# Four normalizations of every 128-row tile issued on ScalarE with scale and bias, and GpSimd computing the bias

## Chip, cores and metric

The kernel runs on one core of a Trainium2 chip. The metric is the device time of one launch in microseconds (us). The engines are named as in the profile: PE is TensorE (PEld its weight loads), DVE is VectorE, ACT is ScalarE, POOL is GpSimd, SP is SyncE, which here issues all DMAs.

## What is computed

One transformer layer over x of shape 16 x 1024 x 256, with two residual branches, each closed by a layer norm without weights:

```
x = x + layernorm(attention(layernorm(x)))     # 16 heads of 16, relative-position scores, softmax over 1024 keys
x = x + layernorm(ffn(layernorm(x)))           # base + shared rank 16 + 6 routed experts of rank 16, top 2 by softmax
layernorm(x) = (x - mean(x)) / sqrt(var(x) + 1e-5)    # over the 256 columns
```

So there are four normalizations for each row: before attention (xn here), after attention (yn), before the ffn (xn1), after the ffn (y2n).

## The kernel before

Rows are taken in 128 tiles of 128 rows, 8 tiles for each of 16 batches. A tile t of attention runs in 16 **groups** g = 0 to 15: four key blocks jp = g // 4 of 256 keys, and in each four slices i = g % 4 of 32 query rows. A group is a fixed round over the engines:

- PE computes the scores of the group in two halves (`scores`, L662 content term from `qm` and keys, L667 position term from `rm` and the table `tw`). Between the halves it transposes the maxima of the group before (L674).
- DVE takes the maxima (`maxima`, L962, writes r), then reduces the transposed ones (`spread`, L971 writes nm, L974 writes nmm).
- PE then does other work of the tile (`wide`, `mixed`): probabilities times values (L693), transposes (L700, L705), projections (L714), and then subtracts the maximum by a matmul with nmm (`shift`, L683).
- ACT takes the exponential of the shifted scores (`before`, L847), one group later.

The work that belongs to other tiles is hung into these groups at fixed places: the projections of tile n = t + 8, the output projection and first residual of tile t - 1 (a), the ffn of tile t - 2 (b). The order on every engine is written out by hand, and semaphores join them; each engine works strictly in its own order. The prologue projects 8 tiles without attention, the main loop is unrolled over 3 tiles (42 passes, so 126 tiles), and two short tiles close.

POOL's order in one tile (function `tile` of the gpsimd block) is, from group 12 on: bias add of y (L612) and y2 (L615), `rstd` for rs1 and rs3 (L541 to L543: variance plus eps, then the power -0.5, on one column), the residual x1 (L625), `mask(0)`, `rstd` for rs2, `mask(1)`, `mask(2)`, the output residual res (L641), and in the next tile `mask(3)`, the fp16 splits of x1T and xT (L547, L549), `rstd` for rs0, the products wp of the attention parts with their weights (L580) and their sums (L588, L590), the bias add qkb (L594) and the split into qkh and qkl (L547, L549). `mask(i)` (L534, L535) prepares `qm` and `rm` of the next tile; PE asks for it before the scores of group i.

DVE's side work (`side`) holds, besides the statistics (L923, L925), the four normalizations `normal` (L928), a tensor_scalar that subtracts the mean and multiplies by rs: xn in group 3, yn in 13, y2n in 14, xn1 in 15. In group 5 it holds the gate of the ffn's router, among it L1005 (gate), L1010 (ceq) and L1011 (cgt).

What asks for the four results: PE transposes xn and xn1 in group 0 (L705), POOL adds yn in x1 and y2n in res, and SP loads the next x tile once xn is written.

Of the kernel before, what the change touches and what calls it, by code (L numbers as in the profile page):

```python
# [13 lines left out]
P = 128  # L14
# [24 lines left out]
def sandwich_kernel(nc, x, wqT, bq, wkT, bk, wvT, bv, woT, bo, relT, baseT, base_b,  # L39
                    shAT, shBT, roAT, roBT, rtT, rtb, out):  # L40
    f32, f16 = mybir.dt.float32, mybir.dt.float16
    ALU = mybir.AluOpType
    ACT = mybir.ActivationFunctionType
# [9 lines left out]
    with ctx:  # L53
        def sb(name, shape, dt=f32):
            return ctx.enter_context(nc.sbuf_tensor(name, shape, dt))
# [11 lines left out]
        tri = sb("tri", [P, E, E])  # L67
        mhalf = sb("mhalf", [P, 1])
        eps = sb("eps", [P, 1])
        one = sb("one", [P, 1])  # L70
# [48 lines left out]
        xin = sb("xin", [P, D])  # L119
        xn = sb("xn", [P, D])  # L120
# [3 lines left out]
        mv0 = sb("mv0", [P, 2])  # L124
        ve0 = sb("ve0", [P, 1])
        rs0 = sb("rs0", [P, 1])
        qkf = sb("qkf", [P, 4, P])
        qkb = sb("qkb", [P, 4, P])
# [7 lines left out]
        y = sb("y", [P, D])  # L136
# [8 lines left out]
        ve1 = sb("ve1", [P, 1])  # L145
        rs1 = sb("rs1", [P, 1])
        st2 = sb("st2", [P, 6])
        mv2 = sb("mv2", [P, 2])
        ve2 = sb("ve2", [P, 1])
        rs2 = sb("rs2", [P, 1])  # L150
        st3 = sb("st3", [P, 6])
        mv3 = sb("mv3", [P, 2])
        ve3 = sb("ve3", [P, 1])
        rs3 = sb("rs3", [P, 1])
        hf = sb("hf", [P, NH])
        lg = sb("lg", [P, E])
# [333 lines left out]
        def _(pool):  # L490
# [7 lines left out]
            g.memset(tri[:, :, :], 1.0)  # L498
            g.memset(mhalf[:, :], -0.5)
            g.memset(eps[:, :], EPS)  # L500
            g.memset(one[:, :], 1.0)
# [37 lines left out]

            def rstd(dst, mv, ve):  # L540
                g.tensor_tensor(ve[:, :], mv[:, 1:2], eps[:, :], ALU.add)  # L541
                pool.drain()
                return g.tensor_tensor(dst[:, :], ve[:, :], mhalf[:, :], ALU.pow)  # L543

# [12 lines left out]
            def tile(t, n, att, proj, a, b, ph=None):  # L557
# [12 lines left out]
                if proj:  # L570
                    pool.wait_ge(s_xT, n + 1)
                    split([flat(xT2[:, k, :, :]) for k in range(2)], flat(xT[:, :, :]), s_xT2)

                    pool.wait_ge(s_mv0, n + 2)
                    rstd(rs0, mv0, ve0).then_inc(s_rs0, 1)
                if a:
# [39 lines left out]
                if a:  # L616
                    pool.wait_ge(s_mv1, t)
                    rstd(rs1, mv1, ve1).then_inc(s_rs1, 1)
                if b:
                    pool.wait_ge(s_mv3, t - 1)  # L620
                    rstd(rs3, mv3, ve3).then_inc(s_rs3, 1)
                if a:
# [8 lines left out]
                if a:  # L631
                    pool.wait_ge(s_mv2, t)
                    rstd(rs2, mv2, ve2).then_inc(s_rs2, 1)
                if att:
# [8 lines left out]
            pool.wait_ge(s_mv0, 1)  # L643
            rstd(rs0, mv0, ve0).then_inc(s_rs0, 1)
            passes(pool, tile)


# [185 lines left out]
        def _(act):  # L833
# [4 lines left out]
            def copy(dst, src):  # L838
                return A(dst, src, ACT.Copy)  # L839

            def exp(g, buf, count, free):

                jp, i = divmod(g, NI)
                act.wait_ge(s_shift, count)
                if not (isinstance(free, int) and free <= 0):
                    act.wait_ge(s_pv, free)
                A(prob[:, jp % 2, :, :, i * IW:(i + 1) * IW],  # L847
                  sc[:, 2 * buf:2 * buf + 2, :].rearrange("p c (h i) -> p c h i", i=IW),
                  ACT.Exp).then_inc(s_exp, 1)

            def before(g, t, ph):

                pg = (g - 1) % NG
                exp(pg, buffer(ph, g - 1), t * NG + g, (t - 1 if g == 0 else t) * NJP + pg // NI - 1)

            def tile(t, n, att, proj, a, b, ph=None):
                for g in range(NG):
# [55 lines left out]
                    if a if g == 0 else att:  # L913
                        before(g, t, ph)

            passes(act, tile)


        @block.vector
        def _(dve):  # L920
# [6 lines left out]
            def normal(dst, src, mv, rs):  # L927
                return v.tensor_scalar(dst, src, mv[:, 0:1], rs[:, 0:1], ALU.subtract, ALU.mult)  # L928
# [48 lines left out]
            def side(g, t, n, proj, a, b):  # L977
# [9 lines left out]
                if g == 2 and proj:  # L987

                    dve.wait_ge(s_x, (n + 1) * 16)
                    stats(st0, mv0, xin[:, :]).then_inc(s_mv0, 1)  # L990
                if g == 3 and proj:
                    dve.wait_ge(s_rs0, n + 2)
                    dve.wait_ge(s_xTp, n + 1)
                    normal(xn[:, :], xin[:, :], mv0, rs0).then_inc(s_xn, 1)
                if g == 4 and b:
# [54 lines left out]
                if g == 13 and b:  # L1050
                    dve.wait_ge(s_y2, t - 1)
                    stats(st3, mv3, y2[:, :]).then_inc(s_mv3, 1)
                if g == 13 and a:
                    dve.wait_ge(s_rs1, t)
                    normal(yn[:, :], y[:, :], mv1, rs1).then_inc(s_yn, 1)
                if g == 14 and a:
                    dve.wait_ge(s_x1, t)
                    stats(st2, mv2, x1[:, :]).then_inc(s_mv2, 1)
                if g == 14 and b:
                    dve.wait_ge(s_rs3, t - 1)  # L1060
                    normal(y2n[:, :], y2[:, :], mv3, rs3).then_inc(s_y2n, 1)
                if g == 15 and a:
                    dve.wait_ge(s_rs2, t)
                    normal(xn1[:, :], x1[:, :], mv2, rs2).then_inc(s_xn1, 1)

# [43 lines left out]
```

## Time and profile before

| | |
|---|---|
| time, median of 3 runs | 6342.19 us (6337.41 to 6345.55) |
| the profiled execution | 6342.86 us |
| its span | 6341.1 us |
| busy: PE, DVE, POOL, ACT | 94%, 79%, 58%, 49% |
| mean granted TensorE clock | 0.985 |

The span is the time from the first to the last recorded instruction; 1.8 us of the execution lie outside it. Rows of the trace are given as start in us, duration in us, engine, line, operation, output <- inputs, shapes and count; a bracket at the end is the time in which the engine stood idle just before, and what ended it.

### The profile page before, as it was taken

Reading aid. Unit: us, or ns where it says so; the run is one execution under the profiler, and the core shown is the slowest. Engines: PE = TensorE matmul, PEld = TensorE weight load, DVE = VectorE, ACT = ScalarE, POOL = GpSimd, SP = SyncE. Lnnn points to the kernel's source line nnn. Section 1 sums busy time; section 2 is a strip of 40 time slices with the busy share of each in tenths; the row PEclk is TensorE's granted clock in tenths of the full one; section 3 lists DMA queues with packets and bytes.
Section 4 is the critical chain, followed back from the end, with each engine's and each line's share of the span. In section 5 each row is a group of like instructions: output and inputs, shape, how many; then the busy total and the mean of one; then the engine's idle time right before and its main releaser. Section 6 shows DMA issues by size and latency. Waiting matters only on the chain.

```text
span 6341.1 us, 408511 instructions
## 1 busy us (share of the span) xinstructions
PE 5961.8 (94%) x178176; PEld 5617.6 (89%) x178176; DVE 4987.0 (79%) x10289; ACT 3127.8 (49%) x5145; POOL 3652.9 (58%) x4709
## 2 busy tenths in 40 slices
PE   5999999999999999999999999999999999999997
PEld 4989899899998998898999899899999999998987
DVE  3787788878788887878887888888788788887786
ACT  1555455455555554555555555455555555554554
POOL 5555655565565555555655655555565556556555
PEclk7999999999999999999999999999999999999998
DMA  3111121111212112121121211112111121211211
GB/s 87 39 44 52 36 61 36 54 44 38 60 36 62 36 36 62 36 61 34 42 58 36 60 37 49 47 40 60 36 53 45 36 60 40 59 37 36 62 36 27
DMA packets 570090, 296.74 MB, mean 47 GB/s; under 512 B 384177, under 2 KB 534689, under 8 KB 568625
## 3 DMA queue, kind: packets, MB, share of 16 engines
q1 hardware_dynamic: 568624, 272.86, 16.0%
q8 instruction: 1450, 23.76, 1.6%
q14 instruction: 16, 0.12, 0.0%
HBM read 184.46 MB, written 88.60 MB: 43 GB/s over the span
## 4 chain that ended last, share of the span: by engine, by line
PE 83%; DVE 8%; issue 4%; DVEq 3%; POOLq 1%; ACT 1%; POOL 0%; SPq 0%; DMA 0%
PE sc L667 22%; PE pw L693 15%; PE sc L683 14%; PE sc L662 13%; PE pm L714 4%; PE pw L700 4%; PE pw L714 4%; PE pm L674 4%; DVE r L962 3%; DVEq L973 2%; DVE y2n L928 2%; DVE nm L971 1%; PE pm L727 1%; PE pm L705 1%; DVE gate L1005 1%
## 5 line engine op out<-in xcount | busy, mean ns | idle before, releaser
L962 DVE TRANSPOSE_TENSOR_REDUCE r<-sc 128x32 f16<-128x1024 f32 x2048 | 2548.8, 1245 | 52.0 <-PE sc L667 51.4
L667 PE MATMUL sc<-rm,tw 96*128 96x32 f16 x65536 | 2293.4, 177 | 71.6 <-issue 70.8
L847 ACT ACTIVATE prob<-sc 128x1024 f32<-128x1024 f32 x2048 | 2097.3, 1024 | 193.7 <-PE sc L683 141.3
L667 PEld LDWEIGHTS sc<-rm,tw 96*128 96x128 f16 x65536 | 1979.9, 97 | 79.5 <-issue 79.0
L662 PE MATMUL sc<-qm,ks 96*128 96x64 f16 x32768 | 1639.8, 193 | 28.8 <-DMA ks<-qk_s 15.5
L971 DVE TENSOR_REDUCE nm<-pm 16x32 f16<-16x256 f32 x2048 | 840.8, 411 | 753.7 <-PE pm L674 750.3
L662 PEld LDWEIGHTS sc<-qm,ks 96*128 96x128 f16 x32768 | 1302.8, 98 | 34.3 <-issue 34.2
L683 PE MATMUL sc<-nmm,pick 128*128 128x64 f16 x32768 | 1302.0, 193 | 2.5 <-DVE nmm L974 1.2
L683 PEld LDWEIGHTS sc<-nmm,pick 128*128 128x128 f16 x32768 | 1151.9, 98 | 122.4 <-issue 105.5
L693 PE MATMUL pw<-prob,vs 128*32 128x128 f32 x32768 | 1115.7, 277 | 129.8 <-DVE nm L971 124.7
L693 PEld LDWEIGHTS pw<-prob,vs 128*32 128x32 f32 x32768 | 842.6, 110 | 185.8 <-DVE nm L971 137.4
L974 DVE TENSOR_TENSOR nmm<-nm,mask_h 16x64 f16<-16x64 f16 x2048 | 607.6, 297 | 195.1 <-issue 9.8
L839 ACT ACTIVATE ot<-pw 128x512 f32<-128x512 f32 x512 | 305.8, 597 | 739.7 <-PE pw L693 739.7
L547 POOL TENSOR_TENSOR oT<-oT,one 128x256 f16<-128x256 f32 x128 | 78.6, 614 | 926.9 <-ACT oT L839 926.9
L535 POOL TENSOR_TENSOR rm<-raw,mask_r 96x512 f16<-96x512 f16 x515 | 608.3, 1181 | 0.0
L534 POOL TENSOR_TENSOR qm<-raw,mask_q 96x512 f16<-96x512 f16 x515 | 591.3, 1148 | 20.3 <-PE sc L667 10.4
L674 PE MATMUL pm<-ident,r 128*128 128x128 f16 x4096 | 561.5, 218 | 0.5 <-DVE r L962 0.5
L839 ACT ACTIVATE nmt<-pm 128x16 f32<-128x16 f32 x512 | 94.2, 184 | 771.1 <-PE pm L727 771.1
L700 PE MATMUL pw<-ident,ot 128*128 128x128 f32 x2048 | 322.9, 280 | 54.2 <-DVE nm L971 53.9
L839 ACT ACTIVATE parts<-pw 128x272 f32<-128x272 f32 x512 | 203.5, 397 | 327.2 <-PE pw L700 320.6
L580 POOL TENSOR_TENSOR wp<-parts,wst 128x1088 f32<-128x1088 f32 x128 | 281.6, 2200 | 113.3 <-ACT parts L839 113.3
L543 POOL TENSOR_TENSOR rs<-ve,mhalf 128x1 f32<-128x1 f32 x521 | 287.4, 552 | 74.0
(131 smaller groups left out, 5803.9 us busy)
## 6 DMA issues: line engine op xcount, KB each, us to landing
raw<-qk_s SPq DMA_DIRECT2D x774, 64.0 KB, 2.8
tw<-tw_s SPq DMA_DIRECT2D x512, 72.0 KB, 2.1
v_s<-vpad SPq DMA_DIRECT2D x136, 256.0 KB, 3.6
vs<-v_s SPq DMA_DIRECT2D x64, 512.0 KB, 3.7
ks<-qk_s SPq DMA_DIRECT2D x384, 64.0 KB, 2.5
xin<-x SPq DMA_DIRECT2D x138, 128.0 KB, 2.9
qk_s<-qkh SPq DMA_DIRECT2D x272, 64.0 KB, 1.7
qk_s<-qkl SPq DMA_DIRECT2D x272, 64.0 KB, 1.6
```

The source lines that it names most:

```text
L534: g.tensor_tensor(qm[:, i, :, :], src, mask_q[:, :, :], ALU.mult)
L535: g.tensor_tensor(rm[:, i, :, :, :].rearrange("p i h s -> p h i s"), src.rearrange("p h (i s) -> p h i s", s=2), mask_r[:, :, :].rearrange ...
L662: last = mm(bank[:, 2 * h * IW:(2 * h + 2) * IW], ks[:, h, j:j + P], qm[:, i, 2 * h:2 * h + 2, :].rearrange("p h i -> p (h i)"), start=(h ...
L667: last = mm(out3[:, :, 2 * k:2 * k + 2], tw[:, jp, u:u + P], rm[:, i, k, :, :], start=False, stop=False, skip_group_check=True)
L674: last = mm(p_max[:, c * P:(c + 1) * P], r1[:, c * H:c * H + P], ident16[:, :], start=True, stop=True)
L683: last = mm(pairs[:, :, h, :], pick[:, h, :], nmm[:, :, :], start=False, stop=True, skip_group_check=True)
L693: last = mm(pw[32 * q:32 * q + 32, col * P:(col + 1) * P], vs[:, 2 * jp + c, h, :], prob[:, jp % 2, c, h, :], start=(c == 0), stop=(c == 1))
L839: return A(dst, src, ACT.Copy)
L847: A(prob[:, jp % 2, :, :, i * IW:(i + 1) * IW], sc[:, 2 * buf:2 * buf + 2, :].rearrange("p c (h i) -> p c h i", i=IW), ACT.Exp).then_inc(s ...
L962: v.tensor_reduce(r1[:, 0:2 * H], sc[:, 2 * buf:2 * buf + 2, :].rearrange("p c (h i) -> p (c h) i", i=IW), axis=AX.X, op=ALU.max, apply_tr ...
L971: v.tensor_reduce(part, p_max[0:H, :].rearrange("h (q i) -> h i q", i=IW), axis=AX.X, op=ALU.max, negate=True).then_inc(s_nmr, 1)
L974: v.tensor_tensor(nmm[0:H, :, :], part.rearrange("h (a i) -> h a i", a=1) .to_broadcast((H, 2, IW)), mask_h[:, :, :], ALU.mult).then_inc(s ...
```

## The change

The four `normal` calls leave DVE and become ACT activations `Identity(scale * x + bias)` with scale = rs and bias = nb, both one column of 128 partitions. Since nb = -mean * rs must be known, the helper `rstd` on POOL now has four instructions in place of two: ng = mean * -1 beside the variance plus eps, and after the power a second drain and nb = ng * rs. Its semaphore is raised after nb. The first normalization of all, ahead of the prologue, stays on DVE. On ACT each normalization stands at the end of its group, behind the exponential.

```
             def rstd(dst, mv, ve, ng, nb):
                 g.tensor_tensor(ve[:, :], mv[:, 1:2], eps[:, :], ALU.add)
+                g.tensor_tensor(ng[:, :], mv[:, 0:1], minus[:, :], ALU.mult)
                 pool.drain()
-                return g.tensor_tensor(dst[:, :], ve[:, :], mhalf[:, :], ALU.pow)
+                g.tensor_tensor(dst[:, :], ve[:, :], mhalf[:, :], ALU.pow)
+                pool.drain()
+                return g.tensor_tensor(nb[:, :], ng[:, :], dst[:, :], ALU.mult)
...
+            def normal(dst, src, rs, nb):          # scalar block
+                return A(dst, src, ACT.Identity, scale=rs[:, 0:1], bias=nb[:, 0:1])
...
                     if a if g == 0 else att:
                         before(g, t, ph)
+                    if g == 3 and proj:
+                        act.wait_ge(s_rs0, n + 2)
+                        act.wait_ge(s_xTp, n + 1)
+                        normal(xn[:, :], xin[:, :], rs0, nb0).then_inc(s_xn, 1)
+                    if g == 13 and a:
+                        act.wait_ge(s_rs1, t)
+                        normal(yn[:, :], y[:, :], rs1, nb1).then_inc(s_yn, 1)
+                    if g == 14 and b:
+                        act.wait_ge(s_rs3, t - 1)
+                        normal(y2n[:, :], y2[:, :], rs3, nb3).then_inc(s_y2n, 1)
+                    if g == 15 and a:
+                        act.wait_ge(s_rs2, t)
+                        normal(xn1[:, :], x1[:, :], rs2, nb2).then_inc(s_xn1, 1)
...
-                if g == 13 and a:                  # vector block; the other three likewise
-                    dve.wait_ge(s_rs1, t)
-                    normal(yn[:, :], y[:, :], mv1, rs1).then_inc(s_yn, 1)
```

On POOL, from the statistics of y2 (group 13) to mask(1), the third tile of the loop before (names: x is the residual x1; ve, rs carry the number of their norm in the code):

```order
L541 TENSOR_TENSOR ve<-mv,eps 128x1
L543 TENSOR_TENSOR rs<-ve,mhalf 128x1
L625 TENSOR_TENSOR x<-yn,xr 128x256
...
L534 TENSOR_TENSOR qm<-raw,mask_q 96x512
L535 TENSOR_TENSOR rm<-raw,mask_r 96x16x16x2
L541 TENSOR_TENSOR ve<-mv,eps 128x1
L543 TENSOR_TENSOR rs<-ve,mhalf 128x1
```

and the same place of the changed kernel:

```order
L551 TENSOR_TENSOR ve<-mv,eps 128x1
L552 TENSOR_TENSOR ng<-mv,minus 128x1
L554 TENSOR_TENSOR rs<-ve,mhalf 128x1
L556 TENSOR_TENSOR nb<-ng,rs 128x1
L638 TENSOR_TENSOR x<-yn,xr 128x256
...
L544 TENSOR_TENSOR qm<-raw,mask_q 96x512
L545 TENSOR_TENSOR rm<-raw,mask_r 96x16x16x2
L551 TENSOR_TENSOR ve<-mv,eps 128x1
L552 TENSOR_TENSOR ng<-mv,minus 128x1
L554 TENSOR_TENSOR rs<-ve,mhalf 128x1
L556 TENSOR_TENSOR nb<-ng,rs 128x1
```

Two instructions more stand ahead of x1 and two more ahead of mask(1); two more still, not shown, stand ahead of wp in the next tile.

On DVE, groups 13 and 14 of the same tile before:

```order
L923 BN_STATS st<-y 128x6
L925 BN_AGGR mv<-st 128x2
L928 TENSOR_SCALAR yn<-y,mv,rs 128x256
L971 TENSOR_REDUCE nm<-pm 16x32
L974 TENSOR_TENSOR nmm<-nm,mask_h 16x64
L961 REGISTER_ALU
L962 TENSOR_REDUCE r<-sc 128x32
L923 BN_STATS st<-x 128x6
L925 BN_AGGR mv<-st 128x2
L928 TENSOR_SCALAR y2n<-y,mv,rs 128x256
```

and on ACT, groups 13 to 15 of the changed kernel, where they have gone:

```order
L863 ACTIVATE prob<-sc 128x32x32
L855 ACTIVATE yn<-y,nb,rs 128x256
L852 ACTIVATE ot<-pw 128x512
L860 REGISTER_ALU
L863 ACTIVATE prob<-sc 128x32x32
L855 ACTIVATE y2n<-y,nb,rs 128x256
L852 ACTIVATE parts<-pw 128x272
L860 REGISTER_ALU
L863 ACTIVATE prob<-sc 128x32x32
L855 ACTIVATE xn<-x,nb,rs 128x256
```

The three normalizations stand between ACT's exponentials and its copies out of PSUM; here xn is the buffer xn1.

## Rows read from the trace of the kernel before

**Rows 1.** The page: the chain that ended last, shares by engine.

```profile
PE 83%; DVE 8%; issue 4%; DVEq 3%; POOLq 1%; ACT 1%; POOL 0%; SPq 0%; DMA 0%
```

**Rows 2.** Waits of PE over the whole span: total us, times, longest.

```profile
PE pw L693 <- DVE nm L971: 124.7, 126, 1.1
...
PE pw L700 <- DVE nm L971: 53.9, 127, 0.5
```

**Rows 3.** Timeline of PE, group 15 to group 6 of the next tile; ACT in group 15.

```profile
3055.11 0.66 PE L700 MATMUL pw<-ident,ot 128*128 128x128 f32 x4 [0.40 <-DVE nm L971]
...
3057.71 0.38 PE L705 MATMUL pm<-ident,xn 128*128 128x128 f32 x2
...
3058.39 0.40 PE L662 MATMUL sc<-qm,ks 96*128 96x64 f16 x8
...
3075.87 1.08 PE L693 MATMUL pw<-prob,vs 128*32 128x128 f32 x32 [1.05 <-DVE nm L971]
...
3056.27 1.02 ACT L847 ACTIVATE prob<-sc 128x1024 f32<-128x1024 f32 x1
```

**Rows 4.** Timeline of DVE in the same stretch.

```profile
3054.04 0.68 DVE L928 TENSOR_SCALAR y2n<-y,mv,rs 128x256 f32<-128x256 f32 x1
...
3068.49 1.03 DVE L974 TENSOR_TENSOR nmm<-nm,mask_h 16x64 f16<-16x64 f16 x1
...
3073.73 0.41 DVE L1005 TENSOR_SCALAR gate<-eg,rg 128x6 f32<-128x6 f32 x1
...
3074.34 1.15 DVE L1011 TENSOR_TENSOR cgt<-gate 128x36 f32<-128x36 f32 x1
3075.41 0.41 DVE L971 TENSOR_REDUCE nm<-pm 16x32 f16<-16x256 f32 x1
```

**Rows 5.** Timeline of POOL in the same stretch.

```profile
3050.70 0.27 POOL L541 TENSOR_TENSOR ve<-mv,eps 128x1 f32<-128x1 f32 x1 [1.71 <-DVE mv L925]
3051.11 0.55 POOL L543 TENSOR_TENSOR rs<-ve,mhalf 128x1 f32<-128x1 f32 x1
3051.63 0.73 POOL L625 TENSOR_TENSOR x<-yn,xr 128x256 f32<-128x256 f32 x1
...
3056.54 1.27 POOL L535 TENSOR_TENSOR rm<-raw,mask_r 96x512 f16<-96x512 f16 x1
...
3066.04 0.19 POOL L541 TENSOR_TENSOR ve<-mv,eps 128x1 f32<-128x1 f32 x1
...
3067.25 2.24 POOL L580 TENSOR_TENSOR wp<-parts,wst 128x1088 f32<-128x1088 f32 x1 [0.32 <-ACT parts L839]
...
3073.08 1.04 POOL L547 TENSOR_TENSOR qkh<-qkb,one 128x512 f16<-128x512 f32 x1 [0.20 <-issue]
3074.27 1.17 POOL L549 TENSOR_TENSOR qkl<-qkb,qkh 128x512 f16<-128x512 f32 x1
```

**Rows 6.** Timelines of the next tile, behind the loop's back edge: PE, then POOL.

```profile
3106.23 0.44 PE L667 MATMUL sc<-rm,tw 96*128 96x32 f16 x11 [1.22 <-issue]
...
3115.24 0.19 POOL L541 TENSOR_TENSOR ve<-mv,eps 128x1 f32<-128x1 f32 x1 [1.96 <-DVE mv L925]
...
3117.59 2.16 POOL L580 TENSOR_TENSOR wp<-parts,wst 128x1088 f32<-128x1088 f32 x1 [1.47 <-ACT parts L839]
```

**Rows 7.** Groups by line: busy us, mean ns, idle before.

```profile
L580 POOL TENSOR_TENSOR wp<-parts,wst 128x1088 f32<-128x1088 f32 x128 | 281.6, 2200 | 113.3 <-ACT parts L839 113.3
...
L839 ACT ACTIVATE y<-pm 128x256 f32<-128x256 f32 x256 | 98.4, 384 | 316.5 <-PE pm L714 316.5
...
L839 ACT ACTIVATE nmt<-pm 128x16 f32<-128x16 f32 x512 | 94.2, 184 | 771.1 <-PE pm L727 771.1
...
L888 ACT ACTIVATE eg<-lg,nlm 128x6 f32<-128x6 f32 x128 | 37.2, 291 | 0.5 <-DVE nlm L999 0.5
```

**Rows 8.** Timelines where POOL is idle: DVE in the last tile, POOL in the prologue.

```profile
6327.93 0.19 DVE L1011 TENSOR_TENSOR cgt<-gate 128x36 f32<-128x36 f32 x1
...
58.81 1.04 POOL L594 TENSOR_TENSOR qkb<-qkf,b_qk 128x512 f32<-128x512 f32 x1 [2.67 <-ACT qkf L839]
```

More of the change, by code:

```diff
@@ L68, in sandwich_kernel @@
         mhalf = sb("mhalf", [P, 1])
+        minus = sb("minus", [P, 1])
         eps = sb("eps", [P, 1])
@@ L126, in sandwich_kernel @@
         rs0 = sb("rs0", [P, 1])
+        ng0 = sb("ng0", [P, 1])
+        nb0 = sb("nb0", [P, 1])
         qkf = sb("qkf", [P, 4, P])
@@ L146, in sandwich_kernel @@
         rs1 = sb("rs1", [P, 1])
+        ng1 = sb("ng1", [P, 1])
+        nb1 = sb("nb1", [P, 1])
         st2 = sb("st2", [P, 6])
@@ L150, in sandwich_kernel @@
         rs2 = sb("rs2", [P, 1])
+        ng2 = sb("ng2", [P, 1])
+        nb2 = sb("nb2", [P, 1])
         st3 = sb("st3", [P, 6])
@@ L154, in sandwich_kernel @@
         rs3 = sb("rs3", [P, 1])
+        ng3 = sb("ng3", [P, 1])
+        nb3 = sb("nb3", [P, 1])
         hf = sb("hf", [P, NH])
@@ L499, in _ @@
             g.memset(mhalf[:, :], -0.5)
+            g.memset(minus[:, :], -1.0)
             g.memset(eps[:, :], EPS)
@@ L538, in mask, with rstd @@
                                 ALU.mult).then_inc(s_mask, 1)
-            def rstd(dst, mv, ve):
+            def rstd(dst, mv, ve, ng, nb):
                 g.tensor_tensor(ve[:, :], mv[:, 1:2], eps[:, :], ALU.add)
+                g.tensor_tensor(ng[:, :], mv[:, 0:1], minus[:, :], ALU.mult)
                 pool.drain()
-                return g.tensor_tensor(dst[:, :], ve[:, :], mhalf[:, :], ALU.pow)
+                g.tensor_tensor(dst[:, :], ve[:, :], mhalf[:, :], ALU.pow)
+                pool.drain()
+                return g.tensor_tensor(nb[:, :], ng[:, :], dst[:, :], ALU.mult)
             def split(two, whole, inc):
@@ L574, in tile @@
                     pool.wait_ge(s_mv0, n + 2)
-                    rstd(rs0, mv0, ve0).then_inc(s_rs0, 1)
+                    rstd(rs0, mv0, ve0, ng0, nb0).then_inc(s_rs0, 1)
                 if a:
@@ L617, in tile @@
                     pool.wait_ge(s_mv1, t)
-                    rstd(rs1, mv1, ve1).then_inc(s_rs1, 1)
+                    rstd(rs1, mv1, ve1, ng1, nb1).then_inc(s_rs1, 1)
                 if b:
                     pool.wait_ge(s_mv3, t - 1)
-                    rstd(rs3, mv3, ve3).then_inc(s_rs3, 1)
+                    rstd(rs3, mv3, ve3, ng3, nb3).then_inc(s_rs3, 1)
                 if a:
@@ L632, in tile @@
                     pool.wait_ge(s_mv2, t)
-                    rstd(rs2, mv2, ve2).then_inc(s_rs2, 1)
+                    rstd(rs2, mv2, ve2, ng2, nb2).then_inc(s_rs2, 1)
                 if att:
@@ L643, in _ @@
             pool.wait_ge(s_mv0, 1)
-            rstd(rs0, mv0, ve0).then_inc(s_rs0, 1)
+            rstd(rs0, mv0, ve0, ng0, nb0).then_inc(s_rs0, 1)
             passes(pool, tile)
@@ L990, in side @@
                     stats(st0, mv0, xin[:, :]).then_inc(s_mv0, 1)
[L991 to L994, printed above, removed]
                 if g == 4 and b:
@@ L1058, in side @@
                     stats(st2, mv2, x1[:, :]).then_inc(s_mv2, 1)
[L1059 to L1064, printed above, removed]
             def tile(t, n, att, proj, a, b, ph=None):
```

## Prediction

> **What bounds the kernel now.** I read the chain that ended last first: PE holds 83% of it, DVE 8% [rows 1]. So PE's own work sets most of the time, and a change elsewhere can act only where PE stands idle or would come to. The waits of PE name two such places that recur in every tile, both on DVE's nm: before the value products L693, 124.7 us in 126 waits (1.0 us each), and before the transposes L700, 53.9 us in 127 (0.42 us each) [rows 2]. The timeline puts L700 into group 15 and the L693 wait into group 6 [rows 3].
>
> What makes DVE late is read on DVE's own rows. In group 14's side work it is y2n, 0.68 us long from 3054.04 [rows 4]; the nm for which PE waits until 3055.11 [rows 3] stands right behind it. In group 5 it is cgt, a 36-element operation that takes 1.15 us and ends at 3075.49; nm follows, and PE goes on at 3075.87 [rows 3, 4]. The same cgt takes 0.19 us in the last tile, where POOL is idle [rows 8]. In the middle of the kernel it ends with POOL's qkl (3074.27 to 3075.44), gate before it ends at 3074.14 with POOL's qkh (3074.12), and nmm at 3069.52 with POOL's wp (3069.49) [rows 4, 5]. So certain DVE operations don't get through while POOL's runs, and DVE's lateness in groups 4 to 6 is that of POOL's queue.
>
> That makes POOL's queue the thing to look at, although POOL is busy only 58% of the span. From the statistics of y2 in group 13 (ve at 3050.70) through x1, three masks, res, mask(3), two splits and rs0 to wp at 3067.25 it is one string of work whose only gap is 0.32 us, ahead of wp, where it waits for ACT's parts [rows 5]. Behind the back edge of the loop PE loses time that nothing shown explains (1.22 us in one piece), and there POOL has gaps of 1.96 and 1.47 us [rows 6]. The mean gap ahead of wp, 113.3/128 = 0.89 us [rows 7], is that of one such tile in three and two tiles with 0.33: (84 x 0.33 + 42 x 2.0)/128 = 0.87. So 84 tiles have 0.33 us of slack in POOL's string, and 42 have enough.
>
> **The change, part by part.**
>
> *DVE loses y2n.* With the 0.68 us out of the way nm comes by up to that much earlier, more than the stall of 0.42 us, so the stall goes. Where POOL isn't the bound that is worth 0.42 us a tile; late next is PE itself. The removal of yn, xn1 and xn gives nothing: PE's waits have no entry for them in the loop.
>
> *ACT gains four activations.* An ACT copy of 256 columns takes 384 ns. The operand columns cost something: eg, six columns wide with a bias column, takes 291 ns, nmt, sixteen wide without, 184 ns [rows 7], about 0.115 us a column. Estimate: 0.384 + 2 x 0.115 = 0.61 us each, between 0.38 and 0.70. ACT is busy 49% and idles around the exponentials, so 2.4 us more a tile fit in. The tightest is xn1, behind the exponential of group 14: PE's second pair of L705 at 3057.71 [rows 3] would be asked for at 3057.31 once the stall is gone, and xn1 would be written at about 3057.5 (the exponential at 3056.27 [rows 3] comes 0.4 earlier and ends at 3056.89, then 0.61). That is a wait of 0.2 us and hides behind the next item. By the Trainium skill (ScalarE: Activation LUTs, What ACT_TABLE_LOAD costs) an ACTIVATE takes 186 ns + 0.833 ns an element and 93 ns more for each column operand, 0.585 us here; with it the sum stays as it is.
>
> *POOL gains two small instructions and one drain in each rstd, and this is the term that decides.* In rs3, ve takes 0.27 us and rs starts 0.41 us after it, so a drain costs 0.14; rs takes 0.55; the ve of rs0 takes only 0.19 [rows 5]. After rs the next instruction starts 0.52 us on (3051.11 to 3051.63), an overlap of 0.03. ng beside ve adds 0.19 - 0.03 = 0.16. nb adds 0.14 + 0.19 = 0.33. Together e = 0.49 us for each rstd. The bounds: 0.33 if ng disappears in ve's shadow; 0.62 if each small operation runs as the ve at 3050.70 did (0.27 us). I take 0.49, the row without neighbours on DVE. Three of the four rstd (rs3, rs2, rs0) lie in the string; rs1 lies before it, where POOL has an idle 1.71 us [rows 5].
>
> Two consumers feel it. First mask(1), whose rm ends at 3057.81, against the scores of group 1 at 3058.39 [rows 3, 5]: slack 0.58, less 0.05 for the semaphore. It moves by 2e = 0.98, so with PE 0.4 earlier it is late by 0.85, and PE starts group 1 0.45 later than before: the 0.42 won in group 15 is lost here and 0.45 more. Then wp moves by 3e = 1.47 less the slack of 0.33, that is 1.14 us. nmm of group 3 would be asked for 0.45 later, at 3068.94, while wp then starts at about 3068.4, so it still runs into wp and waits for its end. From there gate, cgt and nm follow POOL's qkh and qkl as before, and PE leaves the wait of group 6 1.14 us later. This closes a loop: PE from there to group 13 works without a wait, and POOL's string begins anew. So each of the 84 tiles costs 1.14 us and the win in group 15 is swallowed: 84 x 1.14 = +96 us. In the 42 tiles behind the back edge POOL's gaps (1.96 and 1.47) take the delay, and the win stays: 42 x -0.42 = -18 us.
>
> The Trainium skill has a rule that speaks for the change (SBUF — State Buffer, Who interferes with whom): DVE and GpSimd share a port pair that one instruction holds to its end, and PE and ACT wait on no one. By it y2n on ACT is free of that lock, and the 0.42 us of each tile would be won. The rows of y2n and cgt agree with the lock; they don't say that POOL's queue has room.
>
> *The rest.* The prologue: POOL waits 2.67 us for ACT's qkf ahead of qkb [rows 8], and rs0 with its nb fits into that; ACT's xn is written before qkf is ready. 0 us; without that cover 8 x 0.5 = 4 us. The last two tiles are drained, every rstd is on the path: 4 x 0.49 = +2 us. SP loads x tiles one tile ahead and sees xn 1 to 2 us later, nothing.
>
> Sum: 96 - 18 + 2 = +80 us on the profiled execution's 6342.86, 6423; that execution stands 0.7 us above the median, so **6422 us** against the median, 1.3% slower.
>
> **The rivals.**
>
> *Faster: POOL's queue isn't binding.* If the additions cost less than a third of the slack (3e < 0.33, e < 0.11), or if DVE's blocked operations slip ahead of POOL's in the new order, the win of group 15 remains in each tile: 127 x -0.42 = -53 us, 6289. For it: DVE and not POOL is named in both waits. Against: a drain alone costs 0.14 us, and the string has one gap. The lock rule of the SBUF page gives this time. 12%.
>
> *Only the mask wait.* POOL's wp is late, but nmm and cgt find gaps, so that the delay of wp isn't passed to PE; what is left is group 1: 84 x 0.45 - 18 + 2 = +22 us, 6364. It needs nmm to be asked for before wp starts; the distance is 0.5 us at e = 0.49 and is used up only at e about 1.0. 8%.
>
> *More than one wait.* xn1 or yn comes too late on ACT, or further nmm run into POOL's masks, so that PE waits in groups 0 to 3 in all tiles, the ones behind the back edge too. From 0.2 us a tile on it shows; at 0.5 x 126 it adds 63 us: 6485. For it: nmm has several POOL instructions around it. Against: PE's shift comes 0.3 us or more after nmm in most groups. 6%.
>
> **How the numbers follow.** The main case has 74%. Its own range: e from 0.33 to 0.62 gives 84 x (3e - 0.33) = 55 to 129 us, less 16: 6382 to 6456. The range given reaches down to the mask case and up towards the case of more waits: 6355 to 6485, leaving out the faster case (12%) and a tail above (5%). A difference of 0.2% is about what a measurement of this kernel can tell. Slower: 74 + 8 + 6, less a few for small e: 84%. Faster: 12%. Same: 4%.
>
> **What would show each step.** Right: PE's wait before L700 gone; a new wait of PE's scores L662 on POOL's rm (group 1) in two tiles of three; the wait of L683 on nmm or L693 on nm grown; POOL's gap ahead of wp gone in 84 tiles; periods from wp to wp of about 48.4 instead of 47.25 us in these; POOL busy up by 8 x 128 x 0.19 = 195 us; ACT activations of 0.6 us. Wrong if cgt becomes short, if POOL's string still has its gap, or if the back-edge tiles grow too.

## The result and the profile after

| | before | after |
|---|---|---|
| time, median | 6341.91 us (6337.41 to 6345.55, 4 runs) | 6383.99 us (6372.15 to 6389.37, 4 runs) |
| the profiled execution, its span | 6342.86, 6341.1 us | 6389.37, 6387.6 us |
| mean granted TensorE clock | 0.985 | 0.985 |

The changed kernel is slower: ratio 1.0064, 95% interval 1.0047 to 1.0082, +42 us. The forecast was +80. The granted clock is the same, so it has no part in the difference.

The page of the changed kernel, first the line of busy times, then the shares of the chain that ended last:

```profile
PE 6011.2 (94%) x178176; PEld 5631.9 (88%) x178176; DVE 4892.3 (77%) x9769; ACT 3392.8 (53%) x5665; POOL 3764.4 (59%) x5752
...
PE 73%; issue 9%; POOL 6%; POOLq 5%; DVE 4%; DVEq 2%; ACT 1%; SPq 0%; DMA 0%; ACTq 0%
```

POOL and its sequencer together now hold 11% of the chain where they held 1% [rows 1], although POOL is still busy for only 59% of the span. The waits of PE (us in total, times, longest):

```profile
PE pw L706 <- DVE nm L1000: 140.5, 127, 1.2
...
PE sc L675 <- POOL rm L545: 29.1, 85, 0.4
...
PE sc L675 <- issue: 23.4, 42, 1.0
```

L706 is the L693 of before, L675 its L662, L680 its L667, L713 its L700, L718 its L705. The 53.9 us of the wait at L700 [rows 2] are gone. In their place stand a new wait of 29.1 us for POOL's mask, 85 times, and 15.8 us more in group 6. The last row was 13.2 us before.

The timeline of the changed kernel, two stretches of one tile: group 13 to the scores of group 1, and groups 3 to 6. All engines are in one list, in order of start:

```profile
3020.43 0.19 POOL L551 TENSOR_TENSOR ve<-mv,eps 128x1 f32<-128x1 f32 x1 [1.23 <-DVE mv L954]
3020.57 0.19 POOL L552 TENSOR_TENSOR ng<-mv,minus 128x1 f32<-128x1 f32 x1
...
3020.90 0.55 POOL L554 TENSOR_TENSOR rs<-ve,mhalf 128x1 f32<-128x1 f32 x1
...
3021.59 0.19 POOL L556 TENSOR_TENSOR nb<-ng,rs 128x1 f32<-128x1 f32 x1
...
3021.80 0.73 POOL L638 TENSOR_TENSOR x<-yn,xr 128x256 f32<-128x256 f32 x1
...
3024.32 0.66 PE L713 MATMUL pw<-ident,ot 128*128 128x128 f32 x4
...
3024.72 0.19 POOL L551 TENSOR_TENSOR ve<-mv,eps 128x1 f32<-128x1 f32 x1
...
3026.02 1.16 POOL L544 TENSOR_TENSOR qm<-raw,mask_q 96x512 f16<-96x512 f16 x1
...
3026.46 0.59 ACT L855 ACTIVATE xn<-x,nb,rs 128x256 f32<-128x256 f32 x1
3026.80 0.42 PE L718 MATMUL pw<-ident,xn 128*128 128x128 f32 x2
...
3027.13 1.16 POOL L545 TENSOR_TENSOR rm<-raw,mask_r 96x512 f16<-96x512 f16 x1
...
3027.19 0.41 PE L718 MATMUL pm<-ident,xn 128*128 128x128 f32 x2
...
3028.42 0.41 PE L675 MATMUL sc<-qm,ks 96*128 96x64 f16 x8 [0.35 <-POOL rm L545]
...
3037.67 0.19 POOL L556 TENSOR_TENSOR nb<-ng,rs 128x1 f32<-128x1 f32 x1
...
3037.81 2.04 POOL L593 TENSOR_TENSOR wp<-parts,wst 128x1088 f32<-128x1088 f32 x1
...
3038.47 1.42 DVE L1003 TENSOR_TENSOR nmm<-nm,mask_h 16x64 f16<-16x64 f16 x1
...
3044.64 1.17 POOL L562 TENSOR_TENSOR qkl<-qkb,qkh 128x512 f16<-128x512 f32 x1
3044.71 1.15 DVE L1036 TENSOR_TENSOR cgt<-gate 128x36 f32<-128x36 f32 x1
3045.78 0.41 DVE L1000 TENSOR_REDUCE nm<-pm 16x32 f16<-16x256 f32 x1
3046.24 1.08 PE L706 MATMUL pw<-prob,vs 128*32 128x128 f32 x32 [1.24 <-DVE nm L1000]
```

Read it from the top. L713 has no bracket any more: y2n is off DVE and the stall of group 15 is gone. The second pair of L718 starts 0.39 us after the first, where before the two stood 0.26 apart (3057.45 and 3057.71): it transposes xn1, which ACT has ready only at 3027.05. The rstd at 3024.72 holds POOL for 1.30 us until qm, where before it took 0.89 (3054.54 to 3055.43). rm ends at 3028.29, and the scores of group 1 wait 0.35 us for it: that is the new wait. wp starts with no bracket, POOL's gap of 0.32 us [rows 5] is used up. nmm again ends with wp (3039.89 and 3039.85), cgt with qkl (3045.86 and 3045.81), and PE waits 1.24 us in group 6 where it waited 1.05 [rows 3].

The groups by line (busy us, mean ns, idle before) give the size of what was added:

```profile
L554 POOL TENSOR_TENSOR rs<-ve,mhalf 128x1 f32<-128x1 f32 x521 | 286.3, 550 | 74.0
L593 POOL TENSOR_TENSOR wp<-parts,wst 128x1088 f32<-128x1088 f32 x128 | 261.0, 2039 | 52.9 <-ACT parts L852 52.9
L556 POOL TENSOR_TENSOR nb<-ng,rs 128x1 f32<-128x1 f32 x521 | 99.0, 190 | 74.1
L552 POOL TENSOR_TENSOR ng<-mv,minus 128x1 f32<-128x1 f32 x521 | 98.0, 188 | 0.0
```

ng and nb are 188 and 190 ns long. POOL's idle time ahead of wp fell from 113.3 us [rows 7] to 52.9, and wp itself from 2200 to 2039 ns.

Over the whole run I took the distances between starts of wp. Two tiles stand ahead of the loop, so its 42 passes have 84 distances within a pass and 41 across the back edge. Before, the means within a pass are 47.37 and 47.25 us, across the back edge 50.40; after, 47.99, 48.03 and 50.02. So 42 x (0.62 + 0.78) = +59 us in the tiles in the middle and 41 x -0.38 = -15 us behind the back edge. Out of the loop the last distance grew from 46.59 to 49.05 and the rest behind the last wp from 37.3 to 39.3, and 1.0 us was won ahead of the loop: +3.5. Together that is the difference of the spans (46.5).

### The profile page after: what moved, and what is told of

The parts are those of the page before. It is cut to its first block, busy times and chain, and to the rows that moved or that the text cites. A ratio compares the mean times of both kernels' runs of the same rounds, so it can differ in the third digit from the quotient of the medians.

```text
span 6387.6 us, 409991 instructions
## 1 busy us (share of the span) xinstructions
PE 6011.2 (94%) x178176; PEld 5631.9 (88%) x178176; DVE 4892.3 (77%) x9769; ACT 3392.8 (53%) x5665; POOL 3764.4 (59%) x5752
## 4 chain that ended last, share of the span: by engine, by line
PE 73%; issue 9%; POOL 6%; POOLq 5%; DVE 4%; DVEq 2%; ACT 1%; SPq 0%; DMA 0%; ACTq 0%
PE sc L680 19%; PE pw L706 13%; PE sc L696 12%; PE sc L675 12%; PE pm L727 4%; PE pw L727 4%; PE pw L713 3%; PE pm L687 3%; POOLq L555 2%; POOLq L553 2%; POOL qm L544 2%; POOL rm L545 2%; DVEq L1002 1%; DVE nm L1000 1%; POOL y L628 1%
## 5 line engine op out<-in xcount | busy, mean ns | idle before, releaser
L680 PE MATMUL sc<-rm,tw 96*128 96x32 f16 x65536 | 2291.8, 177 | 66.7 <-issue 65.2
L680 PEld LDWEIGHTS sc<-rm,tw 96*128 96x128 f16 x65536 | 1980.1, 97 | 73.6 <-issue 72.8
L675 PE MATMUL sc<-qm,ks 96*128 96x64 f16 x32768 | 1643.7, 193 | 67.7 <-POOL rm L545 29.1
L675 PEld LDWEIGHTS sc<-qm,ks 96*128 96x128 f16 x32768 | 1303.2, 98 | 83.7 <-issue 82.9
L706 PE MATMUL pw<-prob,vs 128*32 128x128 f32 x32768 | 1120.3, 278 | 148.3 <-DVE nm L1000 140.5
L706 PEld LDWEIGHTS pw<-prob,vs 128*32 128x32 f32 x32768 | 843.6, 110 | 204.4 <-DVE nm L1000 153.3
L1003 DVE TENSOR_TENSOR nmm<-nm,mask_h 16x64 f16<-16x64 f16 x2048 | 731.4, 357 | 193.6 <-issue 8.2
L545 POOL TENSOR_TENSOR rm<-raw,mask_r 96x512 f16<-96x512 f16 x515 | 593.5, 1152 | 0.0
L713 PE MATMUL pw<-ident,ot 128*128 128x128 f32 x2048 | 323.3, 280 | 0.0
L625 POOL TENSOR_TENSOR y<-y,b_o 128x256 f32<-128x256 f32 x128 | 93.1, 728 | 360.7 <-ACT y L852 360.7
```

Source lines behind the costliest of these rows:

```text
L545: g.tensor_tensor(rm[:, i, :, :, :].rearrange("p i h s -> p h i s"), src.rearrange("p h (i s) -> p h i s", s=2), mask_r[:, :, :].rearrange ...
L675: last = mm(bank[:, 2 * h * IW:(2 * h + 2) * IW], ks[:, h, j:j + P], qm[:, i, 2 * h:2 * h + 2, :].rearrange("p h i -> p (h i)"), start=(h ...
L680: last = mm(out3[:, :, 2 * k:2 * k + 2], tw[:, jp, u:u + P], rm[:, i, k, :, :], start=False, stop=False, skip_group_check=True)
L706: last = mm(pw[32 * q:32 * q + 32, col * P:(col + 1) * P], vs[:, 2 * jp + c, h, :], prob[:, jp % 2, c, h, :], start=(c == 0), stop=(c == 1))
L1003: v.tensor_tensor(nmm[0:H, :, :], part.rearrange("h (a i) -> h a i", a=1) .to_broadcast((H, 2, IW)), mask_h[:, :, :], ALU.mult).then_inc(s ...
```

## The experiments

Three batches, each with its own runs of the kernel before on the same chip: their medians are 6338.66, 6323.32 and 6335.75 us, so times are compared within a batch, as ratios. The differences in us below are those of the medians. The traces of the kernel before that are quoted are those of [rows 1] to [rows 8], from none of these batches; its median fell from 6338.66 to 6323.32 from the first batch to the second, so a trace of the second batch can't be set against them to the last 15 us.

### First batch: the parts alone (before 6338.66 us)

**POOL's part alone.** DVE keeps its four normalizations, nobody reads nb:

```
-                    rstd(rs3, mv3, ve3).then_inc(s_rs3, 1)
+                    rstd(rs3, mv3, ve3, ng3, nb3).then_inc(s_rs3, 1)   # rs0, rs1, rs2 likewise
```

> The POOL half of the change alone: rstd computes ng and nb with its second drain, the four normalizations stay on VectorE as before and don't use nb. Theory A (POOL's string of work from the statistics of y2 to wp is what costs): each rstd takes 0.43 us more, three of them stand in the string, 0.36 us of slack goes off, and the shortenings seen in the changed kernel (rm 1.27 to 1.15, wp 2.24 to 2.04 us) don't come, since VectorE still has its normalizations: 84 tiles x 0.93 = +78 us, and nothing in the 42 tiles behind the back edge; about 6420. Theory B (the loss comes from ScalarE, whose activations take 0.59 us where VectorE took 0.38): no change, 6342, as ScalarE does what it did.

Measured: 6472.31 us, ratio 1.0216 (1.0202 to 1.0230), +134 us. ACT does here what it did before, so its longer activations have no part in this loss. The direction is that of theory A, the size (+78) is not. A small part can be the clock: the five runs have a granted clock of 0.977 to 0.985, those of the kernel before 0.984 to 0.992, and within either kernel 0.001 of clock goes with 1 to 3 us; by that 5 to 18 of the 134 us. Waits of PE in this kernel:

```profile
PE pw L730 <- DVE nm L987: 108.8, 82, 1.3
...
PE pw L709 <- DVE nm L987: 55.2, 111, 1.0
PE pm L721 <- DVE nm L987: 42.7, 85, 1.4
```

and its timeline in group 3 of one tile:

```profile
3078.20 2.04 POOL L596 TENSOR_TENSOR wp<-parts,wst 128x1088 f32<-128x1088 f32 x1
3078.28 2.10 DVE L944 TENSOR_SCALAR xn<-xin,mv,rs 128x256 f32<-128x256 f32 x1
...
3080.77 0.40 PE L730 MATMUL pw<-xT,w_q 128*128 128x128 f16 x4 [1.33 <-DVE nm L987]
```

Here wp follows rs0 without a gap and starts 0.08 us ahead of xn on DVE, which is 0.36 us long where it comes first; it now takes 2.10 and ends 0.14 us behind wp, and the nm behind it stops PE for 1.33 us. The third row, L721, is the same with xn1 in group 0: xn1 meets the whole of POOL's qm (3066.37 to 3067.52), takes 1.22 us instead of 0.37, and PE waits 0.42 us for the nm behind it. The second row is group 6, where the wait fell from 124.7 us to 55.2. The sum of the prediction held only the delay of the queue; where DVE still has xn and xn1, the lateness is handed on once more through the lock.

**The longer rstd off the string.** Only rs1, behind which POOL idles for 1.71 us [rows 5]:

```
-                    rstd(rs1, mv1, ve1).then_inc(s_rs1, 1)
+                    rstd(rs1, mv1, ve1, ng1, nb1).then_inc(s_rs1, 1)
```

> As the run before, but only the rstd for rs1 is lengthened; it stands ahead of an idle 1.7 us of POOL. Theory A (place in the string counts): no difference, within 6 us of before. Rival (each POOL instruction costs, wherever it stands): a quarter of the run before, +20 us. Theory B: no difference.

Measured: 6334.22 us, ratio 0.9996 (0.9987 to 1.0005). The same two instructions and drain, 128 times, cost nothing that can be measured where the queue has room. It is the place that costs, not the instruction.

**y2n alone on ACT**, rs3 long, the rest as before:

```
-                if g == 14 and b:                        # vector block
-                    dve.wait_ge(s_rs3, t - 1)
-                    normal(y2n[:, :], y2[:, :], mv3, rs3).then_inc(s_y2n, 1)
+                    if g == 14 and b:                    # scalar block
+                        act.wait_ge(s_rs3, t - 1)
+                        normal(y2n[:, :], y2[:, :], rs3, nb3).then_inc(s_y2n, 1)
```

> Only y2n goes to ScalarE, with its bias from POOL (rs3 lengthened); the other three norms as before. Theory A: in 84 tiles the string grows by 0.44 less 0.36 of slack, +0.08, which also swallows the stall of 0.42 that goes; in 42 tiles that stall is won: +7 - 18 = -11 us, 6331. Rival (POOL's queue isn't binding, the VectorE stall is all): 127 x -0.42 = -53 us, 6289. Theory B: a quarter of the loss, +10 us.

Measured: 6364.12 us, ratio 1.0042 (1.0029 to 1.0056), +25 us. All three values expected miss (-11, -53 and +10). The stall of group 15 is gone, PE leads by 0.52 and 0.61 us there (medians of the two tiles in the middle of a pass, counted from the value products of group 14); at the shift of group 0 it is 0.41 and 0.37 us behind. Between lies xn1, still on DVE (min, median, max ns of the 128):

```profile
L944 DVE TENSOR_SCALAR xn<-x,mv,rs x128: 597/968/977, 205.4 to 6342.3; 128x256 f32<-128x256 f32 x128
```

Before, its median is 372 ns: DVE came to it (3056.43) just ahead of the end of POOL's qm (3056.58). Here DVE comes earlier and POOL's mask(1), behind the longer rs3, later (3063.86 to 3065.02, xn1 from 3064.20 to 3065.17), so that xn1 is held to the end of qm; nm and nmm of group 15 follow late.

**The bias worked out by ACT**, POOL as before; DVE is rid of all four:

```
+            def negate(ng, mv):
+                A(ng[:, :], mv[:, 0:1], ACT.Copy, scale=-1.0)
+            def bias(nb, ng, rs):
+                A(nb[:, :], ng[:, :], ACT.Copy, scale=rs[:, 0:1])
...
+                    if g == 14 and b:        # ahead of the exponential; group 13 alike, in 15 the bias only
+                        act.wait_ge(s_rs3, t - 1)
+                        negate(ng3, mv3)
+                        act.drain()
+                        bias(nb3, ng3, rs3)
...
+                    if g == 14 and b:        # behind it
+                        act.drain()
+                        normal(y2n[:, :], y2[:, :], rs3, nb3).then_inc(s_y2n, 1)
```

> All four norms on ScalarE, but ScalarE also computes -mean and the bias, with two small activations and drains a norm; POOL is exactly as before. Theory A: the stall of 0.42 us ahead of L700 goes and the wait in group 6 shrinks by the 0.2 us by which wp is shorter without xn beside it; POOL's string has 0.36 + 0.12 us of slack for it: 126 x -0.6 = -75 us, 6267, at worst -40 us if the longer way of xn1 on ScalarE makes PE wait 0.3 us in group 0. Theory B: ScalarE has still more to do than in the changed kernel, so 6384 or slower.

Measured: 6388.17 us, ratio 1.0082 (1.0068 to 1.0095), +50 us. Its waits of PE:

```profile
PE pw L701 <- DVE nm L1022: 116.8, 126, 0.9
...
PE pm L713 <- ACT xn L856: 45.9, 87, 7.0
```

The -75 us expected are missed, and the time is the one that theory B gave (6384 or slower). The wait for the mask is gone, but the small operations in front of the exponential make xn1 late on ACT: the bias for xn1 needs POOL's rs2, for which ACT stands idle 127 times, 0.29 us each, and the exponential behind it waits too. PE then waits for xn1 (0.39 us in the tile that I followed), and at the shift of group 0 it is 0.41 and 0.50 us behind the kernel before. So here ACT is what makes the kernel late. This run doesn't tell whether POOL's lengthening is the cause in the changed kernel; it has a new cause of its own.

### Second batch: smaller parts, and room in POOL's queue (before 6323.32 us)

**xn alone on ACT**, rs0 long:

```
-                if g == 3 and proj:                      # vector block
-                    dve.wait_ge(s_rs0, n + 2)
-                    dve.wait_ge(s_xTp, n + 1)
-                    normal(xn[:, :], xin[:, :], mv0, rs0).then_inc(s_xn, 1)
+                    if g == 3 and proj:                  # scalar block
+                        act.wait_ge(s_rs0, n + 2)
+                        act.wait_ge(s_xTp, n + 1)
+                        normal(xn[:, :], xin[:, :], rs0, nb0).then_inc(s_xn, 1)
```

> Only xn (group 3) goes to ScalarE, with its bias from POOL: rs0 is lengthened, the other three norms and rstd as before. Theory A with the port: rs0 takes 0.43 us more and has 0.36 us of slack ahead of wp; wp, which no longer meets xn on VectorE, takes 2.04 in place of 2.24 us, so nmm, which waits for its end, and all behind it come 0.13 us earlier in 84 tiles and 0.2 us in 42: -19 us, about 6320, with wp at 2.04. Rival (wp's length has another cause): wp stays at 2.24 and the time at +6 us.

Measured: 6310.57 us, ratio 0.9981 (0.9972 to 0.9990), -13 us. wp is 2.04 us long, as in the changed kernel; before, it was 2.16 to 2.24. So DVE's xn, which started just ahead of wp, had held POOL's wp too, and its move gives that back; the prediction had put it at nothing.

**y2n alone on ACT, bias worked out by ACT** behind the exponential, POOL as before:

```
+                    if g == 14 and b:                    # scalar block, behind the exponential
+                        act.wait_ge(s_rs3, t - 1)
+                        negate(ng3, mv3)
+                        act.drain()
+                        bias(nb3, ng3, rs3)
+                        act.drain()
+                        normal(y2n[:, :], y2[:, :], rs3, nb3).then_inc(s_y2n, 1)
```

> Only y2n goes to ScalarE, and ScalarE computes its bias too; POOL has exactly the instructions of before. Theory C (what the stall ahead of L700 gives is taken back because nmm of groups 14 and 15 can't run beside POOL's rm and waits for its end; POOL's string has only some 0.07 us of slack at the shift of group 0): about -0.07 in 84 tiles and -0.42 in 42: -24 us, 6315. Rival (nmm isn't held): 127 x -0.42 = -53 us, 6286. Rival (moving y2n costs as such, as in the run with POOL's bias): +25 us.

Measured: 6313.44 us, ratio 0.9984 (0.9975 to 0.9994), -10 us (4 to 16), less than the -24 of theory C. This is what taking y2n off DVE is worth with POOL untouched: not the 53 us of the stall but 10. The timeline shows where the rest goes:

```profile
2991.16 1.15 POOL L536 TENSOR_TENSOR qm<-raw,mask_q 96x512 f16<-96x512 f16 x1
...
2991.63 0.83 DVE L946 TENSOR_SCALAR xn<-x,mv,rs 128x256 f32<-128x256 f32 x1
...
2992.27 1.20 POOL L537 TENSOR_TENSOR rm<-raw,mask_r 96x512 f16<-96x512 f16 x1
...
2992.88 0.63 DVE L992 TENSOR_TENSOR nmm<-nm,mask_h 16x64 f16<-16x64 f16 x1
...
2993.57 0.64 PE L685 MATMUL sc<-nmm,pick 128*128 128x64 f16 x16 [0.29 <-DVE nmm L992]
```

DVE comes to nmm of group 15 earlier, but POOL's rm runs until 2993.47, and nmm, which takes 0.18 us when free, ends with it (2993.51). The shift of group 0 waits. Before, nmm (3057.52 to 3057.85) ended with rm (3057.81) as well and the shift at 3057.92 just didn't wait. So right behind the stall of group 15 POOL's queue is the bound, with at most 0.07 us of room: PE's lead of 0.52 and 0.61 us in group 15 is down to 0.03 and 0.13 at this shift.

**Room for POOL.** mask(0) moved ahead of the bias add of y2, where POOL would wait, and mask(1) into its old place. It was tried on the changed kernel and on the kernel before:

```
+                if att:                                  # ahead of the bias add of y2
+                    pool.wait_ge(s_raw, t * 96 + 192)
+                    pool.wait_ge(s_scores, t * NG + NG - NI + 1)
+                    mask(0)
...
-                    mask(0)                              # behind x1
+                    pool.wait_ge(s_scores, t * NG + NG - NI + 2)
+                    mask(1)
...
-                    for i in range(1, NI - 1):
+                    for i in range(2, NI - 1):
```

On the changed kernel:

> The changed kernel with POOL's order altered: mask(0) stands ahead of the bias add of y2 (group 12, where POOL is idle 2.6 us), and mask(1) ahead of rstd for rs2. This takes 2.2 us of work out of the string between the statistics of y2 and wp. Theories A and C: POOL binds nowhere, the stall ahead of L700 is gone and wp is shorter: 126 x -0.6 = -76 us on before, 6263; up to 25 us more if nmm meets other POOL work. Rival (the loss is ScalarE's or lies in the number of instructions): about 6384, as the changed kernel.

Measured: 6312.44 us, ratio 0.9981 (0.9972 to 0.9990), -11 us against before; against the changed kernel that is about 50 us. The -76 us expected are missed by far. PE no longer waits for rm. Its lead of 0.52 and 0.61 us from group 15 is still 0.41 and 0.51 at the first pair of L720 (L705 of before) in group 0, and 0.22 and 0.32 at the shift behind the second pair. That pair waits for xn1 on ACT: it starts 0.41 us after the first in place of 0.25 (medians; 95 of 128 tiles lie above 0.33), 0.15 us after the end of xn1. A wait as short as this 0.15 us isn't in PE's list. From there through group 3, where nmm again runs into wp, no more is lost; the lead stays at 0.28 and 0.37. The 41 distances across the back edge are no shorter than before (50.36 us, 50.40 before), and longer than with xn alone on ACT in this batch (49.82).

On the kernel before:

> The kernel before with the same new order on POOL. Theories A and C: the string wasn't what made PE wait there, y2n still meets a mask, so the stall of 0.42 us stays: no difference beyond 15 us, 6340. Together with the run on the changed kernel this says what the change is worth when POOL has room: -60 to -75 us. Rival: the new order alone gives the gain, then both runs come out alike.

Measured: 6351.79 us, ratio 1.0041 (1.0027 to 1.0055), +28 us. The stall of group 15 stays in 84 tiles (0.49 us each), because y2n now meets the whole of POOL's rm and not the second half (before, rm at 3053.43 and y2n at 3054.04). It is DVE that moved: nmm of group 13 starts just ahead of x1 and is through in 0.18 us, where before it met x1 (3051.67, 0.74 us long), so that DVE comes to y2n 0.52 us earlier, while rm starts only 0.09 us later (medians of both tiles in the middle, counted from the value products of group 14). Three rows of the timeline:

```profile
3059.14 0.18 DVE L976 TENSOR_TENSOR nmm<-nm,mask_h 16x64 f16<-16x64 f16 x1
...
3061.00 1.16 POOL L535 TENSOR_TENSOR rm<-raw,mask_r 96x512 f16<-96x512 f16 x1
3061.00 1.30 DVE L930 TENSOR_SCALAR y2n<-y,mv,rs 128x256 f32<-128x256 f32 x1
```

y2n takes 1.30 us here (the median of all 128 too), 0.68 before [rows 4]. The order by itself does harm as long as DVE has y2n, but these rows don't account for the +28: the stall is 0.07 us longer in 84 tiles, and PE waits 13.9 us in 47 places for an nmm. Where the rest arises stays open. With this order the change is worth -39 us (6351.79 to 6312.44), with the old one +42; against the kernel before with its old order it is -11. In either way of counting its sign hangs on POOL's order.

### Third batch: the lock in group 5 (before 6335.75 us)

PE's longest wait, in group 6, stands behind cgt. In these kernels ceq and cgt move from group 5 to the start of group 6, behind nm:

```
+                if g == 6 and b:
                     ge = gate[:, :].rearrange("p (e a) -> p e a", a=1).to_broadcast((P, E, E))
                     gf = gate[:, :].rearrange("p (a f) -> p a f", a=1).to_broadcast((P, E, E))
                     dve.drain()
                     v.tensor_tensor(ceq[:, :, :], gf, ge, ALU.is_equal)
                     v.tensor_tensor(cgt[:, :, :], gf, ge, ALU.is_gt)
-                if g == 6 and b:
                     dve.drain()
```

**On the kernel before:**

> The kernel before, with the router's two comparisons (ceq, cgt) moved from group 5 to the start of group 6 on VectorE, where they come after POOL's qkl. Theory A (PE's wait ahead of L693 is cgt held by qkl): nm starts when gate is through, at the end of qkh; the wait of 1.05 us in group 6 all but goes, less some 0.2 us for the comparisons in group 6: 126 x -0.85 = -107 us. Rival (the wait has another cause): no change.

Measured: 6270.19 us, ratio 0.9897 (0.9882 to 0.9912), -66 us. The wait of group 6 is gone from the list; part of it comes back at the transposes:

```profile
PE pw L700 <- DVE nm L971: 97.2, 244, 0.5
```

244 times in place of 127: besides group 15 there is now the L700 of group 7, for which nm comes 0.37 us late in 119 tiles. These 44 us are what is missing to the -107 expected.

**On the changed kernel:**

> The changed kernel with the same move. Theory A: POOL's later qkl is no longer passed on to PE, so the wait of 1.24 us goes too, at 126 x -0.9 = -115 us on the changed kernel; against before -70. If the loss of 42 us of the change came through qkl alone, this run and the one on the kernel before would come out alike; if part of it comes through group 0 and 1 (theory C: nmm behind rm, and the scores behind mask(1)), this one stays slower by 20 to 40 us.

Measured: 6294.82 us, ratio 0.9934 (0.9921 to 0.9948), -41 us. Less than the -70 expected, but it stays 24.6 us behind the one above, within the 20 to 40 of theory C. So the change costs in this kernel too, and its waits of PE say where:

```profile
PE pw L713 <- DVE nm L1000: 54.7, 120, 0.6
PE sc L675 <- POOL rm L545: 29.1, 85, 0.3
```

The wait for the mask is the same 29.1 us: it doesn't depend on what happens in group 6.

**Changed kernel, early masks and late comparisons:**

> The changed kernel with both moves, the early masks on POOL and the late comparisons on VectorE. Theories A and C: the gains add, -11 measured for the masks with the change, and -107: about -118 us on before, below the kernel before with late comparisons alone by 10 to 40 us. Rival (either is hidden by the other): as the better of the two alone.

Measured: 6228.02 us, ratio 0.9832 (0.9818 to 0.9845), -108 us: the fastest of all, and faster than both kernels of the case; 42 of the 108 us are won on the kernel before with late comparisons alone. The kernel before with both moves wasn't run, so what the change is worth in this order isn't measured. The waits of PE on other engines that recur in every tile have come down to this row:

```profile
PE pw L715 <- DVE nm L1002: 25.9, 120, 0.2
```

The 0.15 us for xn1 on ACT, too short for this list, is there here too: the second pair of L720 starts 0.41 us after the first in most tiles.

**The same with only y2n and xn on ACT**, yn and xn1 back on DVE, and rs1 and rs2 short:

> Both moves, but only y2n and xn on ScalarE, yn and xn1 on VectorE as before; POOL computes a bias in rs3 and rs0 only. These are the two normalizations from which something was won (the stall ahead of L700, the length of wp). By theory the string is shorter by 0.4 us and xn1 takes the shorter way: equal to the run with all four on ScalarE or up to 20 us faster.

Measured: 6277.48 us, ratio 0.9916 (0.9903 to 0.9930), 49 us behind the one with all four. I had expected it level or ahead. First PE's waits, then xn1 (min, median, max ns):

```profile
PE pw L714 <- DVE nm L995: 27.8, 118, 0.4
...
PE sc L697 <- DVE nmm L998: 25.9, 89, 0.7
```

```profile
L952 DVE TENSOR_SCALAR xn<-x,mv,rs x128: 472/966/972, 202.1 to 6254.3; 128x256 f32<-128x256 f32 x128
```

xn1 on DVE is held by POOL's mask again, and nmm behind it. So the moves of xn1 and yn to ACT, which the prediction had put at nothing, carry a good part of what the change is worth; the rows show xn1's part, yn's can't be told from them.

## Why it was slower, and why by less than forecast

**The mechanism** came as put on record: the wait of group 15 gone, a new wait of group 1 on rm in two tiles of three (85 times), POOL's gap ahead of wp gone, the wait of group 6 longer, the tiles behind the back edge shorter. Four runs bear on the cause. The longer rstd costs 134 us by itself, with ACT as it was, and nothing where only rs1 has it, off the string; with room made in POOL's queue the same change wins 39 us, or 11 against the kernel before. That also disposes of the rival by which POOL's queue isn't binding (6289), and of the rule of the Trainium skill (SBUF — State Buffer, Who interferes with whom) taken by itself: the lock is there (nmm, gate and cgt end 0.02 to 0.05 us behind POOL's operation, the held ones of 256 columns 0.14 to 0.15), but a rule on one pair of instructions says nothing about the queue in which one of them stands.

**The steps by their numbers.**

- *e, the lengthening of an rstd:* forecast 0.49 us. rs2 went from 0.89 to 1.30, rs3 from 0.93 to 1.37, rs0 from 0.88 to 1.31: 0.41, 0.44 and 0.43, together 1.28 instead of 1.47. The instructions are 0.19 long as forecast, but the next one starts 0.14 to 0.15 after the start of the one before.
- *POOL's own instructions got shorter:* not in the sum. rm of mask(1) went from 1.27 [rows 5] to 1.16, -0.11; wp from 2.24 to 2.04, -0.20. POOL had been held by DVE as DVE by POOL. The run with xn alone on ACT shows this for wp: 2.04, and -13 us.
- *A tile in the middle:* forecast 3e - 0.33 = 1.14 us. Measured +0.62 and +0.78. From the parts: 1.28 - 0.11 - 0.20 - 0.33 = 0.64. Over the 84 tiles +59 us in place of +96: **this is the term that was mis-sized**, by 0.50 us a tile from its parts: 0.19 by e, 0.31 because the shorter wp and rm were not foreseen.
- *Behind the back edge:* forecast -0.42, measured -0.38, so -15 us in place of -18. PE's waits without a releaser grew at L675 from 13.2 to 23.4 us, and fell at L680 from 70.8 to 65.2: 4.6 us more in all. What lies behind them stays open.
- *The ends:* forecast +2, measured +4.4 behind the loop and -1.0 ahead of it.
- *The mask wait:* forecast 0.45 us beyond the 0.42 that were won; PE waits 0.35 and is 0.28 and 0.19 us later than before at that point, in the two tiles in the middle of a pass.
- *ACT:* 0.59 us an activation for the estimated 0.61. By an estimate from the figures of the Trainium skill (ScalarE: Activation LUTs, What ACT_TABLE_LOAD costs) it is 0.585 us; the trace agrees, with 591 ns. The feared 0.2 us of wait for xn1 came, as 0.15: its transposes start 0.41 us behind the pair before them instead of 0.25, 0.15 us after xn1 is written. In the changed kernel it hides in front of the wait for the mask, as forecast; in the kernels with early masks PE pays for it.
- *POOL's busy time:* forecast +195 us, measured +111 (3652.9 to 3764.4). ng and nb add 197; wp gives back 21 by the rows, ve 19 (mean 225 to 188 ns), rm 15 (1181 to 1152 ns), and ng overlaps ve by 0.05 us, 521 times, or 26: 116.

**What was wrong inside the right direction.** I took the 0.42 us of the stall for a gain that only the longer rstd takes away. The run with y2n alone on ACT and POOL untouched won 10 us, not 53: nmm and xn1 stand against mask(0) and mask(1), and the room at the shift of group 0 was at most 0.07 us, not the 0.5 to which the prediction came by looking at group 1 alone. "The removal of yn, xn1 and xn gives nothing" was wrong too: xn gave 13 us, and xn1 together with yn 49 us in the last batch. An entry in PE's list of waits is missing as long as another wait stands ahead of it; it is no proof that an operation is free. That the time came within the range owes something to the width of the range: +42 is half of +80, and what was left out, the shorter wp and rm, happened to pull one way.

**Left open.** How the 49 us of the last run divide between xn1 and yn; an nmm that doesn't meet POOL's masks, and the kernel before with both moves, which weren't tried; and where the order by itself loses 28 us.

## What to carry to other kernels

Where two engines lock each other out as here, their orders form one queue: before moving work between them, or lengthening an instruction on the one, write down for each operation on the path what runs on the other at that moment and when it ends, since a short operation takes as long as the long one that it meets. Busy share says nothing there (POOL at 58% set the time); what counts is where the gaps of its queue lie, and an edit that costs 0.4 us three times ahead of the only gap of 0.33 is paid but for that gap, while the same edit ahead of a gap of 1.7 is free. Then look at the order first: moving two masks and two comparisons turned +42 us into -108, though 66 of these come with the comparisons alone, without the change.

## What was not expected of the hardware

- The lock acts both ways in the same pair: with DVE's xn started just ahead of it, wp takes 2.16 to 2.24 us, with xn on ACT 2.04. rm of mask(1) goes likewise from 1.27, with xn1 on DVE started 0.11 us ahead of it, to 1.16.
- A tensor_scalar of fp32 that reads one 256-column tensor and two single columns is held too: xn1 takes 0.37 us where it comes late in a mask's qm or free, and 0.97 to 1.22 where it comes earlier, xn 0.36 and, beside wp, 2.10.
- Of small POOL instructions without a drain between them the next starts 0.14 us after the one before, though each is recorded as 0.19 us long; a drain and the next dependent one start 0.14 us after the recorded end.
